# The first bf16 part of the negated row maxima written by ScalarE beside the f32 value, GpSimd's first cast left out, and the planner's tables of ranks made anew

## The reference, cut to what matters

```python
def _attn(q, k, v):
    scores = jnp.einsum('bqhd,bkhd->bhqk', q, k) * scale
    w = jax.nn.softmax(scores, axis=-1)
    out = jnp.einsum('bhqk,bkhd->bqhd', w, v)
```

## Time and profile before

| | us |
|---|---|
| median of 3 runs | 2919.24 (2916.59 to 2923.46) |
| time of the profiled execution | 2916.84 |
| its span, first to last instruction | 2915.0 |
| mean granted TensorE clock | 0.976 of full |

### The profile page before, as it was taken

The page is one execution under the profiler, slowest core; times in us unless marked ns, Lnnn a source line. Parts: engine busy times, 40 slices in busy tenths (PEclk is TensorE's granted clock), DMA queues, the critical chain, the costliest instruction groups (busy, mean ns, idle before and its releaser), DMA issues. The chain is left out here.

```text
span 2915.0 us, 47676 instructions
## 1 busy us (share of the span) xinstructions
PE 2728.5 (94%) x15136; PEld 1351.8 (46%) x15136; DVE 1893.7 (65%) x4209; ACT 1425.8 (49%) x2579; POOL 590.3 (20%) x999
## 2 busy tenths in 40 slices
PE   8999999999989999999988888898999999999899
PEld 5444344335544424334455566656645323224456
DVE  5977388642574783866344889668974884885621
ACT  3455635574445583566644444333221674785441
POOL 2110001131331110331125323411020010112510
PEclk9999999999999999999998999999999999999899
DMA  6333122433452312233066516521420322123621
GB/s 207 69 104 107 41 72 71 112 89 98 144 172 53 114 51 67 91 115 95 22 186 186 167 50 195 146 85 60 147 60 1 116 60 52 45 61 108 183 92 38
DMA packets 268153, 286.78 MB, mean 98 GB/s; under 512 B 70665, under 2 KB 207243, under 8 KB 267275
## 3 DMA queue, kind: packets, MB, share of 16 engines
q1 hardware_dynamic: 256651, 282.28, 33.0%
q0 software_dynamic: 11264, 1.46, 0.3%
HBM read 167.43 MB, written 114.72 MB: 97 GB/s over the span
## 5 line engine op out<-in xcount | busy, mean ns | idle before, releaser
L1570 ACT ACTIVATE probs<-ring_b 128x512 f32<-128x512 f32 (+1 forms) x1728 | 921.8, 599 | 457.9 <-PE ring_b L1429 359.9
L1748 DVE TENSOR_REDUCE row_max<-ring_a 128x1 f32<-128x1024 f32 x512 | 602.0, 1218 | 151.7 <-PE ring_a L1385 150.9
L1429 PE MATMUL ring_b<-q_ring,k_ring 100*128 100x512 bf16 x1536 | 526.8, 381 | 10.5 <-ACT probs L1570 2.8
L1385 PE MATMUL ring_a<-k_ring,q_ring 96*128 96x512 bf16 x1536 | 450.1, 383 | 27.9 <-DVE row_max L1748 16.1
L1462 PE MATMUL ring_c<-probs,v_and_ones 128*17 128x512 f32 x3072 | 402.0, 599 | 1.8 <-ACT probs L1570 1.2
L1745 DVE CUSTOM_DVE_ANT_0 w_mlp<-ring_a,w_mlp 128x1024 bf16<-128x1024 f32 x256 | 302.1, 1222 | 49.6 <-PE ring_a L1385 48.4
L1868 POOL CAST neg_max_parts<-neg_max 16x128 bf16<-16x128 f32 x112 | 37.6, 336 | 1392.1 <-ACT neg_max L1564 1141.3
L1429 PEld LDWEIGHTS ring_b<-q_ring,k_ring 100*128 100x128 bf16 x1536 | 145.7, 97 | 349.9 <-issue 241.5
L1385 PEld LDWEIGHTS ring_a<-k_ring,q_ring 96*128 96x128 bf16 x1536 | 135.5, 98 | 250.5 <-issue 153.6
L1485 PE MATMUL ring_b<-h_feat,w_mlp 128*128 128x512 f32 x512 | 230.3, 595 | 1.4 <-ACT h_feat L1541 0.8
L1497 PE MATMUL ring_a<-w_mlp 128*128 128x256 f32 x1024 | 226.1, 380 | 5.0 <-DVE w_mlp L1803 2.4
(11 more groups left out here) (143 smaller groups left out, 3346.4 us busy)
## 6 DMA issues: line engine op xcount, KB each, us to landing
q_ring<-scr_q SPq DMA_DIRECT2D x128, 384.0 KB, 4.3
scr_q<-split SPq DMA_DIRECT2D x64, 384.0 KB, 2.6
k_ring<-scr_k SPq DMA_DIRECT2D x64, 384.0 KB, 5.0
scr_q<-split SPq DMA_DIRECT2D x64, 256.0 KB, 3.0
scr_out<-out_stage SPq DMA_DIRECT2D x128, 128.0 KB, 2.5
scr_out<-out_stage SPq DMA_DIRECT2D x64, 256.0 KB, 2.4
h_feat<-scr_out SPq DMA_DIRECT2D x56, 256.0 KB
reciprocals<-scr_recip SPq DMA_DIRECT2D x56, 256.0 KB
```

The costliest lines, as they stand in the source:

```text
L1385: last = mm(ps[:, half * BLOCK:(half + 1) * BLOCK], q[0:PARTS, h, t * P:(t + 1) * P], k_view(g)[0:PARTS, h, half * BLOCK:(half + 1) * BLOC ...
L1429: last = mm(ps[:, :], k_view(g)[0:ROWS, h, s.kt * P:(s.kt + 1) * P], q[0:ROWS, h, q0:q0 + BLOCK], start=not g.masked, stop=True)
L1570: f(PT[0:n, s.pt, :], ps[0:n, :], ACT.Exp, **kw).then_inc(b_evac, 1)
L1748: v.tensor_reduce(NM[:, s.nm, s.u:s.u + 1], ps, AX.X, ALU.max).then_inc(a_evac, 1)
```

## The change

It does three things. ScalarE writes part 0 of the negated maxima in bf16 straight from PSUM, as an instruction of its own ahead of the f32 value, from the same slot of ring b. GpSimd's first cast (L1868) is left out, so three instructions stay. The wait for the MS buffer moves with the first write of it, from GpSimd to ScalarE, and the planner takes the MS buffer ahead of step `max`. Lastly all tables of the planner are new: `RANK`, `REACH`, `SECOND`, `LATER`, and the plan's cost of step `max` on ScalarE (0.125 to 0.4) and of `max_split` on GpSimd (1.64 to 1.34).

```diff
@@ the planner's tables @@
 RANK = dict(
...
-    self_pv=(15, 24, 7.1, 24),
-    self_s=(-9.8, 8.2, -5.8, 8.2),
...
-    win_f=(-6, -12, -4, 0),
-    win_s=(10.5, 8.5, 7.5, 6.5),
...
+    self_pv=(17, 17, 5.8, 5.8),
+    self_s=(-6.8, 6.2, 1.2, 2.2),
...
+    win_f=(5.7, 0.7, -5, 3.8),
+    win_s=(2.5, 7.4, 1.5, 6.5),
 )
-REACH = dict(PE=0.0, ACT=0.0, DVE=0.05, POOL=0.0, SP=0.2)
+REACH = dict(PE=0.0, ACT=0.2, DVE=0.05, POOL=0.05, SP=0.2)
...
-LATER = (-7, -6.5, -5, -40)
+LATER = (-9, -12.5, -13, -40)
@@ -636,10 +636,11 @@
 
     def maxima(g, nm, key):
         nt, nt_last, _ = yield ("get", "NT")
-        s = yield do("max", [("PE", 0.11), ("ACT", 0.125)], after=[g.last_first, nt_last], ring="b", g=g, nm=nm, nt=nt, nt_last=nt_last)
+        ms, ms_last, _ = yield ("get", "MS")
+        s = yield do("max", [("PE", 0.11), ("ACT", 0.4)], after=[g.last_first, nt_last, ms_last], ring="b", g=g, nm=nm, nt=nt, nt_last=nt_last,
+                     ms=ms, ms_last=ms_last)
         p.give("NM", nm, s)
-        ms, ms_last, _ = yield ("get", "MS")
-        d = yield do("max_split", [("POOL", 1.64)], after=[s, ms_last], counts=["msplit_n"], g=g, nt=nt, ms=ms, of=s, ms_last=ms_last)
+        d = yield do("max_split", [("POOL", 1.34)], after=[s], counts=["msplit_n"], g=g, nt=nt, ms=ms, of=s)
         p.give("NT", nt, d)
         s = yield do("max_put", [("POOL", 2.15 if g.edge else 1.67)], after=[d], lat=2.6 if g.cross else 1.9, g=g, ms=ms, of=d)
         g.max_put = s
@@ -1561,6 +1562,9 @@
                     ps = from_b(s.bn)
                     if s.nt_last is not None:
                         act.wait_ge(max_split, s.nt_last.msplit_n + 1)
+                    if s.ms_last is not None:
+                        act.wait_ge(max_in[s.ms_last.g.q], s.ms_last.g.max_need)
+                    f(MS[:, s.ms, 0, :], ps[0:16, 0:P], ACT.Copy, scale=-1.0)
                     f(NT[:, s.nt, :], ps[0:16, 0:P], ACT.Copy, scale=-1.0).then_inc(b_evac, 1)
                 elif s.kind == "score":
                     n = keys_of(s.g)
@@ -1862,10 +1866,7 @@
                     pool.wait_ge(pool_g, s.pool_g + 1)
                 elif s.kind == "max_split":
                     pool.wait_ge(b_evac, s.of.bn + 1)
-                    if s.ms_last is not None:
-                        pool.wait_ge(max_in[s.ms_last.g.q], s.ms_last.g.max_need)
                     r, parts = NT[:, s.nt, :], MS[:, s.ms]
-                    link(g_.tensor_copy(parts[:, 0, :], r))
                     link(g_.tensor_tensor(out=r, in0=r, in1=parts[:, 0, :], op=ALU.subtract))
                     link(g_.tensor_copy(parts[:, 1, :], r))
                     g_.tensor_tensor(out=parts[:, 2, :], in0=r, in1=parts[:, 1, :], op=ALU.subtract).then_inc(max_split, 1)
```

More of the change, by code:

```diff
@@ L283 @@
 RANK = dict(
-    init=(9.3, 10.7, 9.3, 11.3),
-    mod=(2.1, -3, 3.8, 5.8),
-    prep=(4.6, -12, -4, 4.6),
-    out=(-3, -12, -12, -12),
-    ctx=(3.1, 20, 5.1, 7.1),
-    load=(20, -1.2, 0.8, -3.2),
-    cross_f=(11.3, 6.1, 5.7, 3.1),
-    cross_s=(6.3, -1.1, -4.2, 1.0),
-    mlp=(9.0, 8.0, 4.0, -1.4),
-    self_f=(-12, 18.8, -12, 11.8),
-    self_pv=(15, 24, 7.1, 24),
-    self_s=(-9.8, 8.2, -5.8, 8.2),
-    tk=(10.1, 0.1, -12, 9.9),
-    tk_s=(-0.5, 6.1, -9.2, -5.2),
-    win_f=(-6, -12, -4, 0),
-    win_s=(10.5, 8.5, 7.5, 6.5),
+    init=(15.5, 14.6, 14.6, 13.0),
+    mod=(9.8, 5.3, -1.9, 7.3),
+    prep=(5.6, -12, -1, -12),
+    out=(-6, -7, -8, -12),
+    ctx=(9.5, 2.5, 13.1, 2.5),
+    load=(23, 5.3, -0.4, -0.7),
+    cross_f=(10.3, -12, -0.2, 8.3),
+    cross_s=(1.8, 0.8, -9.2, 0.8),
+    mlp=(15.7, 15.7, 3.1, 19.7),
+    self_f=(-7, 16, 16, 16),
+    self_pv=(17, 17, 5.8, 5.8),
+    self_s=(-6.8, 6.2, 1.2, 2.2),
+    tk=(-12, -8, -12, -11),
+    tk_s=(-6, -8, -6, -5),
+    win_f=(5.7, 0.7, -5, 3.8),
+    win_s=(2.5, 7.4, 1.5, 6.5),
 )
-REACH = dict(PE=0.0, ACT=0.0, DVE=0.05, POOL=0.0, SP=0.2)
+REACH = dict(PE=0.0, ACT=0.2, DVE=0.05, POOL=0.05, SP=0.2)
 DELAY = (7.5, 100)
-SECOND = dict(init=-15, mod=-9, prep=-4, out=4, ctx=-24, load=-14, cross_f=7,
-              cross_s=13, mlp=-3, self_f=-3, self_pv=24, self_s=-8, tk=-5, tk_s=-20,
-              win_f=-19, win_s=4)
-LATER = (-7, -6.5, -5, -40)
+SECOND = dict(init=7, mod=5, prep=-22, out=4, ctx=-22, load=-3, cross_f=-7,
+              cross_s=-3, mlp=18, self_f=-1, self_pv=24, self_s=-9, tk=-7, tk_s=-17,
+              win_f=-22, win_s=20)
+LATER = (-9, -12.5, -13, -40)
 FILL_ONE = 0.11
```

## The result

| | before | after |
|---|---|---|
| median of the comparison | 2917.15 us | 2933.44 us |
| ratio, 95% interval | | 1.0057 [1.0046, 1.0068] |
| span of the profiled execution | 2915.0 us | 2925.4 us |
| mean granted TensorE clock | 0.976 | 0.977 |

The changed kernel is slower, by 16.3 us in the medians (0.0057 x 2917 = 16.6). The span of its profiled execution lies 8.0 us under the median, where before it lay 2.1 under. So the two traces show 10.4 of the 16 us. The changed kernel's trace is one of its quicker executions: the granted clock was 0.977 in it, while over its 20 runs it went from 0.969 to 0.978, 0.973 in the middle.

What follows compares the result with a forecast made beforehand. TensorE's list was taken to bound the kernel. Code edit -2 and new order +14 summed to +12 us, so 2931 us against the runs' median of 2919.24; likeliest case 2925 to 2946, 8-in-10 range 2902 to 2952.

Steps and rivals of the forecast that it cites:

- What bounds the kernel: Only TensorE's list sets the time; its idle time plus fillers, 432 us, is all that order can win or lose in.
- The code edit, -2 us: Maxima's chain: cast leaves GpSimd, ScalarE gains an instruction, chain 0.10 us shorter; -2 us taken between -5.4 and +29.
- the bound of 5.4: Largest gain from the code edit: 15 exposed waits at 0.36 us, if all were also behind a queue on GpSimd.
- The new order, +14 us as half of +27.3: New tables thin TensorE's cover by 27.3 us in sum; paid between none and all, half taken, +14 us.
- missing cover: Where TensorE work between a step and its consumer is shorter than the chain's latency, the shortfall, summed: 174.9 to 202.2 us.
- the sum over three chains: Missing cover of maxima to second pass, `out` or `down` to transposition, last `pv` to `out`: +15.0, -3.6 and +15.9 us.
- the latencies in the thin places run beside other bounds: Named failure case: the covers' sum grows by 27 us, yet TensorE's idle time plus fillers stay or fall.
- Waits for the parts above 29.8 us: Sign: TensorE's waits for DMAs of the maxima's parts exceed 29.8 us, growth mostly in layer 2's windows and layer 3.
- +15.9 at `out`: Change in missing cover on the chain from last `pv` to `out`, over all layers, by the new order.
- Rival 2: Whole kernel: no change within 0.2%, 2914 to 2925 us, gains at norms making up for the maxima's chain; chance 0.20.
- Rival 3: Start of layer 2's MLP: ten matmuls fill 8.5 us of idleness and fillers; 2909 us, range 2895 to 2913; chance 0.30.
- Rival 4: ScalarE's wait for the MS buffer, as in cross attention, holds up TensorE: +21 us, about 2952 us; chance 0.10.

Runs made afterwards that it cites:

- the eleventh kernel: Negated maxima in two bf16 parts instead of three, with the chain's edit, in the order of before, against the kernel before: 0.9969 [0.9959, 0.9980].
- the longer chains: GpSimd's next cast written five times instead of once, in the kernel before and in the changed kernel: 1.0199 and 1.0233 of the kernel before.
- experiment 1: Only the chain edited, all engines' lists those of the kernel before, measured twice against it: 0.9987 [0.9973, 1.0001] and 0.9991 [0.9979, 1.0003].
- experiment 2: The changed kernel with cast and buffer wait back on GpSimd, lists those of the change: 1.0088 [1.0068, 1.0109] of the kernel before.
- the order with thick cover: Edited chain with ranks searched from the old tables for a small sum of missing cover: 1.0100 [1.0082, 1.0118] of the kernel before.

## Why the prediction came out right, point by point

**What bounds the kernel.** Nothing speaks against it. GpSimd's 554 us became 414 in the eleventh kernel, and the time fell by 6 us only, while the chain became 0.85 us shorter.

**The code edit, -2 us.** Right in sign and size: -3 us, with an interval that still holds none. Its working was off in two terms, both towards a larger gain. The chain became 0.24 us shorter in the median and 0.18 in the quiet case, not 0.10, because the two ACTIVATEs overlap; and ScalarE grew by 14.9 us, not 29. What the sum did not foresee is that waits only change their cause: 11 to 13 us of waits for the parts went away, and 4.8 us of idle time. In the new order the edit is worth 9 us, 2 to 16 by the intervals, so whether it passes the bound of 5.4 is not settled. That bound counted 15 waits at 0.36 us. The run with the old chain shows 34.1 us of waits for the parts in 20 places, where the changed kernel has 24.6.

**The new order, +14 us as half of +27.3.** The number is right: 2931 us was forecast and 2933.4 measured. For the order that is 16.6 + 3 = 20 with the edit taken out, inside the bounds of 0 and 27, and 6 above the value taken. That the whole came within 3 us is in part luck: the half was taken between two bounds and not worked out, and the longer chains show that it isn't the price of missing cover. There, a maxima's chain that grows beyond its cover is paid for at 0.85 to 0.87 of each us. The order's maxima were covered worse, and about 12 of the 20 us hang on that chain. Wrong is to take the sum over three chains as the measure of an order. An order with 30 us less of it is 32 us slower than the old one with the same chain (0.0111). The sentence of the prediction that names the case, "the latencies in the thin places run beside other bounds", describes it: when the chain gets shorter, TensorE stands for the slots of ring a, for the loads of queries or of `w_gate` instead, and these appear in none of the three sums.

**The signs to look for.** Fillers near 249 us: 249.5. Idle and fillers 444: 443.6. The bf16 ACTIVATE 0.25 to 0.27 us: yes. GpSimd 37 us less: 34.5. ScalarE at 1455 us: 1440.7, since the two ACTIVATEs overlap. Waits for the parts above 29.8 us: wrong, they are 24.6 us. The step that failed is that this sign compares the changed chain with waits of the old one. The edit alone had taken them to 18.5 and 20.0 us; from there the new order raised them by 5, and with the old chain from 31.1 to 34.1. Missing cover behind the maxima had risen by 15. The wait for `h_feat` rose by 8 to 9 us, against +15.9 at `out`; the norm, forecast at -3.6, stayed (22.7 and 22.0 to 23.0). So of the growth that the table has, the maxima show a fifth to a third as waits of TensorE, and `out` about half. Fillers, which rose by 3 to 4 us, can hold more of it.

**Rival 2, no change.** It fell by the interval.

**Rival 3, faster by the start of layer 2's MLP.** A gain is there and is given back. At the first window of layer 2 the changed kernel is 8.0 us late (1488.3 against 1480.3, the first L1390 and L1389), at the last `pv` of the windows level (1857.3 and 1857.2), and at the last top-k transposition 5.9 us late again (2126.5 and 2120.6). Single positions scatter by 5 to 8 us between two traces of one kernel, but the stretch from the first window to the last `pv` is steady: 375.1 to 376.9 us in the three traces with three parts in the order of before (the kernel before and both of experiment 1), 369.0 and 369.5 in the changed kernel and experiment 2. The start of the MLP lies in it; that the 7 us come from just there is not shown. That they would be kept was the error of this rival.

**Rival 4, ScalarE's new wait.** 4.2 us in 3 places. In the order of before, where the plan doesn't hold the step back for the buffer, it is 11.2 us in 6 and 14.9 in 8, and even that cost no time that shows. The Trainium skill, Perfetto Trace Analysis, section on the TensorE instruction, has ScalarE's queue in strict order; no run here tests that.

**What stays open.** Which stage of the order holds the 8 us that the shorter chain did not give back was not isolated. The wait for `h_feat` in layer 2, 6.3 to 7.0 us long in the new order with the old, the new and the short chain alike, is a candidate. But the order of before waits 6.4 to 7.0 us for a norm there, and no run removes either alone. It is open what makes an order slow: no run changes the plan's clock and nothing else. Nor is it settled why the busy time of the order with thick cover is some 19 us above what its fillers explain.

## What to carry to other kernels

Time a code edit in the old order of work first: here it was worth 3 us and the new order that came with it cost 20. A fixed list of steps that was tuned is as much a part of the kernel as its code: none of the six orders planned anew here reached the old one, and the best of them, searched for a short plan, came to 1.0009 against 0.9989.

Latency added to a chain with thin cover was paid almost in full here, latency taken away only as far as the next thing that is late. So a sum of one kind of wait forecasts losses better than gains; before counting on a gain, name what TensorE will wait for next at each place, and compare the whole idle time and not one row of waits.

If a number is only there to be subtracted on both sides of a ratio, ask how many parts of it are needed. Leaving out the third part of the maxima shortened the chain by 0.85 us to its first DMA and was worth some 6 us more, twice the edit.

## What the runs showed of the hardware

Two ACTIVATEs of 16 x 128 elements from PSUM that follow each other start 0.16 to 0.17 us apart though each takes 0.25 to 0.27: 112 more of them added 14.9 us of busy time, not 29.

Waits of TensorE came with slower matmuls. In the longer chain in the old order 34 us of idle time came with 19 us of busy time for the same matmuls and a clock of 0.965 in all five executions, 0.976 before; in the new order 20 us of idle time came with some 20 of busy time, at 0.961 to 0.970 over six executions against 0.969 to 0.978. The scores of the cross attention, right behind the waits, took 454 ns instead of 412. In the window from 2700 to 2800 us, where TensorE was busy for 76 us instead of 86, the granted clock was 0.87 instead of 0.90.

Two executions of one kernel differed by 10.5 us of TensorE's busy time (2723.6 and 2734.1, at 0.978 and 0.975) and not at all in its idle time, 181.7 us in both.
